# A language-model block on one core: the head reordered with all weights early, and the low part of the relu outputs read from PSUM after TensorE has subtracted the high part

## The reference

```
h = tok_W[x] * (x != 0) + pe[0 or 1, or zero for skipped pads]      # (2, 2048, 64)
a = layernorm(h) * g1 + b1;  q, k, v = split(a @ qkv_w + qkv_b)
p = softmax(q @ k.T + rel_bias) * scale                             # over 2048 positions
h = h + layernorm((p @ v) @ proj_w + proj_b) * g2 + b2
z = layernorm(h);  w = softmax over the top 2 of (z @ Wg + bg + bias)
y_e = relu(z @ W1[e] + b1[e]) @ W2[e] + b2[e]       for 8 experts, 64 -> 128 -> 64
out = h + sum_e w_e * y_e
```

## Time and profile before

| | |
|---|---|
| runs shown | 147.24, 149.72, 146.29 us; median 147.24 |
| profiled execution | 145.79 us, span of the trace 144.0 us |
| TensorE matmuls, busy in the span | 106.3 us (74%), 952 instructions |
| VectorE | 110.5 us (77%), 323 |
| ScalarE | 61.0 us (42%), 117 |
| GpSimd | 72.7 us (50%), 90 |

### The profile page before, as it was taken

The page is one execution under the profiler, slowest core; times in us unless marked ns, Lnnn a source line. Parts: engine busy times, 40 slices in busy tenths (PEclk is TensorE's granted clock), DMA queues, the critical chain, the costliest instruction groups (busy, mean ns, idle before and its releaser), DMA issues.

```text
span 144.0 us, 2642 instructions
## 1 busy us (share of the span) xinstructions
PE 106.3 (74%) x952; PEld 59.9 (42%) x952; DVE 110.5 (77%) x323; ACT 61.0 (42%) x117; POOL 72.7 (50%) x90
## 2 busy tenths in 40 slices
PE   0369982698987499699859679299839939829980
PEld 0133731552763276326524346145421624517650
DVE  7799699979407703279999999997999998799623
ACT  2372403103015021897959946276838605640020
POOL 2247928948000530759929995377597630360000
PEclk9999999555555555558999999956985775796555
DMA  3586000000000000000000000010000020003231
GB/s 61 178 282 230 0 2 5 0 1 0 0 0 0 0 7 0 0 2 0 7 0 0 0 5 0 0 36 0 5 0 0 2 41 0 0 0 65 49 73 36
DMA packets 5940, 3.91 MB, mean 27 GB/s; under 512 B 4675, under 2 KB 5031, under 8 KB 5928
## 3 DMA queue, kind: packets, MB, share of 16 engines
q1 hardware_dynamic: 5418, 3.45, 8.5%
q10 hardware_dynamic: 510, 0.31, 1.0%
HBM read 2.70 MB, written 1.06 MB: 26 GB/s over the span
## 4 chain that ended last, share of the span: by engine, by line
DVE 48%; PE 37%; issue 7%; ACT 2%; DMA 2%; POOL 1%; ACTq 0%; DVEq 0%
DVE acc L839 7%; DVE prod L832 5%; PE bank L1114 4%; PE bank L1094 4%; PE bank L1022 3%; PE bank L1019 3%; PE bank L941 2%; DMA w_tok<-in_token_w_dram 2%; DVE xs L798 2%; PE bank L1109 2%; PE bank L1119 2%; PE bank L901 2%; DVE xn L643 2%; DVE xs L797 2%; DVE og L782 2%
## 5 line engine op out<-in xcount | busy, mean ns | idle before, releaser
L324 POOL TENSOR_TENSOR hid_lo<-hid,hid_hi 128x512 f16<-128x512 f32 (+1 forms) x38 | 40.9, 1090 | 22.1 <-ACT hid_hi L570 21.8
L570 ACT ACTIVATE hid<-bank,b_col 128x512 f32<-128x512 f32 (+1 forms) x40 | 25.7, 646 | 26.7 <-PE bank L1094 26.5
L570 ACT ACTIVATE hid_hi<-bank,b_col 128x512 f16<-128x512 f32 (+1 forms) x38 | 24.4, 643 | 0.0
L1094 PE MATMUL bank<-xT,w_hi 128*128 128x512 f16 (+1 forms) x40 | 18.4, 461 | 0.9 <-ACT hid_hi L570 0.8
L839 DVE TENSOR_REDUCE acc<-prod 128x64 f32<-128x512 f32 x18 | 18.5, 1030 | 0.4
L1094 PE MATMUL bank<-xT,w_lo 128*128 128x512 f16 (+1 forms) x40 | 18.6, 465 | 0.0
L832 DVE TENSOR_TENSOR prod<-bank,comb 128x512 f32<-128x512 f32 x18 | 12.4, 688 | 6.3 <-PE bank L1119 5.9
L1114 PE MATMUL bank<-w_hi,hid_hi 128*128 128x64 f16 x144 | 13.6, 212 | 1.7 <-DVE hid_lo L324 1.7
L1114 PEld LDWEIGHTS bank<-w_hi,hid_hi 128*128 128x128 f16 x144 | 11.2, 109 | 7.5 <-issue 5.5
L1114 PE MATMUL bank<-w_lo,hid_hi 128*128 128x64 f16 x144 | 13.6, 212 | 0.0
L1109 PE MATMUL bank<-b_k,ones_b 3*128 3x512 bf16 x18 | 8.6, 476 | 6.6 <-DVE prod L832 5.1
(11 more groups left out here) (217 smaller groups left out, 223.5 us busy)
## 6 DMA issues: line engine op xcount, KB each, us to landing
ids_all<-ids_scratch SPq DMA_DIRECT2D x2, 512.0 KB, 4.6
w_sb<-in_w1g_dram SPq DMA_DIRECT2D x1, 516.0 KB, 6.3
hankel<-in_bias_table_dram SPq DMA_DIRECT2D x1, 512.0 KB, 4.3
out_dram<-looked SPq DMA_DIRECT2D x2, 256.0 KB
out_dram<-fin_all SPq DMA_DIRECT2D x3, 128.0 KB
w_sb<-in_w2b_dram SPq DMA_DIRECT2D x1, 260.0 KB, 6.1
...
```

Source lines behind the costliest of these rows:

```text
L324: return eng.tensor_tensor(hid_lo[:, k % 2, e, 0:m], hid[:, n % HSLOTS, 0:m], hid_hi[:, k % 2, e, 0:m], ALU.subtract)
L570: ins = act.activation(dst, bank[n % 2][:, 0:m], ACT.Relu, bias=b1_col[:, e:e + 1], scale=HSCALE / (XSCALE * XSCALE))
L1094: ins = mm(bank[n % 2][:, 0:m], w[:, HID * e:HID * (e + 1)], xT[:, k % 2, 0:m], start=part == 0, stop=part == 1)
```

## The change

Five things, cut to their core below.

1. The low part of the experts' relu. ScalarE writes the high part first, from the sum in PSUM scaled down by KEEP = 1 - 2^-11 so that it never lies above the full value (`high`). TensorE subtracts it from the same bank by a matmul with a negative scaled identity (`take_high`), and ScalarE applies the relu to what is left in PSUM, in 16 bits (`low`). `hid` and all subtractions of `low` on GpSimd and VectorE go. Each `first_layer(n)` ends with `take_high(n - 1)`, each `hidden(n)` with `low(n - 1)`; three banks are in turn where there were two.
2. The order of the head on TensorE: `project_values` first, `weights` in pieces between the steps of the pair table and unit 0, all four tiles' weights and scores ahead of unit 1's attended values. M_BANK changes so that tiles 2 and 3 have banks 7 and 6.
3. The suffix sums of the skip counts come from 16 matmuls on shifted columns in place of one matmul and a scan.
4. The split of w1: ScalarE scales and rounds it (`w1_high`), GpSimd only subtracts, in four pieces. `bias_parts` works on 8 partitions x 64 in place of 1 x 512, is first on GpSimd, and its result is loaded by three DMAs in place of one.
5. The loads of w1, w2 and b2 go ahead of that of the early ids; `early_one_hots` on VectorE goes from before `split_exps` to after `key_part(1)`.

```diff
-HSLOTS = 6
+KEEP = 1.0 - 2.0 ** -11
+LBANKS = 3
...
-        M_BANK = [7, 2, 2, 2]
+        M_BANK = [7, 2, 7, 6]
...
+            sp.dma_start(w1_sb[:], w1g).then_inc(loads["w1"], 16)
+            sp.dma_start(w2_sb[:], w2b1).then_inc(loads["w2"], 16)
+            sp.dma_start(b2_row[:], b2).then_inc(loads["b2"], 16)
             sp.dma_start(ids_by_seq[:, :, 0:FIRST], ids_dram[:, 0:FIRST].partition_broadcast(P)).then_inc(loads["ids_early"], 16)
-            sp.dma_start(w1_sb[:], w1g).then_inc(loads["w1"], 16)
-            sp.dma_start(b2_row[:], b2).then_inc(loads["b2"], 16)
-            sp.dma_start(w2_sb[:], w2b1).then_inc(loads["w2"], 16)
             sp.wait_ge(s_b2p, 1)
-            sp.dma_start(b2_k[:], b2_part[:]).then_inc(loads["b2_k"], 16)
+            for part in range(3):
+                sp.dma_start(b2_k[part:part + 1, :], b2_part[:, part, :]).then_inc(loads["b2_k"], 16)
...
+            bias_parts(); table_values(); w1_parts(); rsqrt1(0); rsqrt2(0); w2_parts(); rsqrt1(1); rsqrt2(1)
+            rsqrt1(2); rsqrt2(2); rsqrt1(3); rsqrt2(3); fin_parts(0); fin_parts(1); fin_parts(2)
+            fin_parts(3); fin_parts(4); rsqrt1(4); rsqrt2(4)
...
+            def w1_high():
+                act.wait_ge(loads["w2"], 16)
+                act.mul(b1_col[:], w2_sb[:, EXPERTS * D:], HSCALE)
+                act.mul(b1_down[:], w2_sb[:, EXPERTS * D:], HSCALE * KEEP)
+                act.wait_ge(loads["w1"], 16)
+                act.mul(w1_sb[:], w1_sb[:], XSCALE).then_inc(s_w1h, 1)
+                act.wait_ge(s_w1h, 1)
+                act.copy(w1_hi[:], w1_sb[:]).then_inc(s_w1h, 1)
...
+            def high(k, e):
...
                 act.wait_ge(s_z, n + 1)
-                if n >= HSLOTS:
-                    wait_lo(act, n - HSLOTS)
...
+                act.activation(hid_hi[:, k % 2, e, 0:m], bank[n % LBANKS][:, 0:m], ACT.Relu, bias=b1_down[:, e:e + 1],
+                               scale=KEEP * HSCALE / (XSCALE * XSCALE)).then_inc(s_high, 1)
+
+            def low(k, e):
+                n = EXPERTS * k + e
+                act.wait_ge(s_rest, n + 1)
+                m = P * SIZE[k]
+                act.activation(hid_lo[:, k % 2, e, 0:m], bank[n % LBANKS][:, 0:m], ACT.Relu, bias=b1_col[:, e:e + 1],
+                               scale=HSCALE / (XSCALE * XSCALE)).then_inc(s_hid, 1)
+
+            def hidden(k, e):
+                high(k, e)
+                if k or e:
+                    n = EXPERTS * k + e - 1
+                    low(n // EXPERTS, n % EXPERTS)
...
+            read_v(); count_late(0); count_late(1); w1_high(); pair_exps(); read_turned_exps(); squares(0)
+            score_tile(0); score_tile(1); read_turned(0); hidden(0, 0); choice_exp(0); hidden(0, 1); squares(1)
+            hidden(0, 2); score_tile(2); hidden(0, 3); score_tile(3); hidden(0, 4); hidden(0, 5); squares(2)
...
             def read_k():
+                dve.tensor_scalar(minus_h[:], ident[:], -XSCALE * XSCALE / HSCALE, None, ALU.mult)
...
-                link(dve.tensor_tensor_scan(sk_suf[:, ::-1], skc[:, ::-1], skc[:, ::-1], 0.0, ALU.add, ALU.bypass))
-                dve.tensor_scalar(sk_flat[:], sk_suf[:, 1:1 + JBLK], flat, None, ALU.mult)
...
             def flat_weights():
                 dve.wait_ge(s_toe, 1)
                 dve.tensor_scalar(flat_w[:], cnt_half[:, :, 0:2], flat, None, ALU.mult)
+                dve.tensor_scalar(sk_flat[:], sk_suf[:, 1:1 + JBLK], flat, None, ALU.mult)
...
-                link(dve.tensor_copy(hid_hi[:, k % 2, e, 0:P * SIZE[k]], hid[:, n % HSLOTS, 0:P * SIZE[k]]))
-                low_part(dve, k, e).then_inc(s_lo_d, 1)
...
+            one_hot_rows(0, JBLK); skip_blocks(); late_one_hots(); read_k(); toeplitz_low(1); values()
+            read_counts(); skip_columns(); penalties(); flat_weights(); row_maxima()
+            split_exps(); rows_a(0); rows_b(0); rows_b2(0); skip_key(); key_part(0); rows_c(0)
+            skip_key_rows(); key_part(1); early_one_hots(); choose_a(0); choose_b(0); rows_a(1); rows_b(1)
+            rows_b2(1); key_part(2); rows_c(1); key_part(3); rows_a(2); choose_a(1); rows_b(2); rows_b2(2); weigh(0)
...
+                for d in range(ROWS):
+                    ins = mm(bank[1][:, 8:8 + ROWS - d], ones_b[:], skip_j[:, d:], start=d == 0, stop=d == ROWS - 1,
+                             skip_group_check=True)
...
-                if n < 2:
-                    pe_.wait_ge(*((s_idcol, 1), (s_skTsb, 1))[n])
+                if n < LBANKS:
+                    pe_.wait_ge(*((s_idcol, 1), (s_skTsb, 1), (s_p, 2))[n])
                 else:
-                    pe_.wait_ge(s_hid, n - 1)
+                    pe_.wait_ge(s_hid, n + 1 - LBANKS)
...
                 ins.then_inc(s_z, 1)
+                if n:
+                    take_high(n - 1)
+
+            def take_high(n):
+                k, e = n // EXPERTS, n % EXPERTS
+                m = P * SIZE[k]
+                pe_.wait_ge(s_high, n + 1)
+                mm(bank[n % LBANKS][:, 0:m], minus_h[:], hid_hi[:, k % 2, e, 0:m], start=False, stop=True,
+                   skip_group_check=True).then_inc(s_rest, 1)
...
-                if i == 0 and LO_DVE[k]:
-                    wait_lo(pe_, EXPERTS * k + LO_DVE[k][-1])
...
-                if i == 0:
-                    wait_lo(pe_, EXPERTS * k + LO_POOL[k][-1])
...
+            project_values(); counts(); pair_scores(); weights(0, 0, 2); pair_penalties(); weights(0, 2, 4)
+            embed(0); weights(1, 0, 2); turn_exps(); weights(1, 2, 4); attend(0, 2); skip_weights()
+            skip_scores(); scores(0); weights(1, 4, 8); scores(1); weights(3, 0, 4); embed(1); skip_turn()
+            weights(3, 4, 8); turn(0); gate(0); first_layer(0, 0); first_layer(0, 1); attend(2, 4)
+            first_layer(0, 2); weights(2, 0, 2); scores(2); first_layer(0, 3); weights(2, 2, 4); scores(3)
+            first_layer(0, 4); embed(2); first_layer(0, 5); attend(6, 4); first_layer(0, 6); turn(1); gate(1)
+            first_layer(0, 7); first_layer(1, 0); first_layer(1, 1); second_layer(0); first_layer(1, 2)
...
-            first_layer(4, 7); second_layer(14); second_layer(15); second_layer(16); look_up(1)
+            first_layer(4, 7); take_high(EXPERTS * UNITS - 1); second_layer(14); second_layer(15); second_layer(16); look_up(1)
```

117 lines of the change are left out of this document (35 added, 82 removed).

## The result

| | before | after |
|---|---|---|
| median of the runs | 147.09 us (4 runs, 146.29 to 149.72) | 128.36 us (4 runs, 127.58 to 132.16) |
| after to before | | 0.8725, 95% interval 0.8633 to 0.8816 |
| span of the profiled execution | 144.0 us | 125.6 us |
| mean granted clock over the span | 0.740 | 0.919 |

The kernel is faster by 12.8%. The forecast was 124.0 in a range of 114 to 136; the time lies in it, 4.4 us above the forecast. The four executions of the kernel after run from 127.58 us at a mean clock of 0.919 to 132.16 at 0.875; where the clock touches a comparison, the text gives it.

The account below looks back on a forecast made before the run. The prediction took TensorE at half clock to bound B and VectorE, stretched by GpSimd's subtractions, to bound C. Gains of 3.3 + 9.0 + 9.7 + 1.0 = 23.0 us gave a span of 121.0, forecast as 124 us, range 114 to 136.

Parts of the forecast that it names:

- Stage A: From the start until VectorE starts the variance of unit 0, 28.2 us; 3.3 us gained, bounds 0 and 5.
- L710's stall: Before the penalties, a multiply took 2.17 us behind GpSimd's split of w1; some 2.0 of it would go.
- The cover for `w1_high`: ScalarE's 7.15 us of idle before the exponentials would hide its 3 us of new work, under 1 us to spare.
- Stage B: From unit 0's variance until TensorE turns unit 1: TensorE work at half rate, 32.0 us to 23.0, 9.0 gained.
- The clock check: A sign for stage B: granted clock above 0.8 between the scores and turn(1), with turn(1) near 48.
- rival 1: The head stays at the lower clock level: stage B gives 0 instead of 9.0, about 133 us; chance 15%.
- Stage C: From TensorE turning unit 1 until VectorE weighs block 14, bound by VectorE: 70.2 us to 60.5, 9.7 gained.
- the coupling: In stage C, two nearly full engines, VectorE and TensorE, coupled by 18 handovers lose some: 4 us added.
- rival 4: TensorE keeps at the upper clock level in stages C (54 us) and D (10 us): about 115 us; chance 13%.
- Rival 2, the ring,: An expert's high, take_high and low run one after another, 2.6 us an expert: 145, or 150 to 170; chance 6%.
- Rival 3: VectorE does not get faster without GpSimd, the long rows having another cause: about 132 us; chance 6%.
- Stage D: From VectorE weighing block 14 to the end, 13.6 us; 1.0 us gained, bounds 0 and 4.7.

Follow-up runs that it names:

- run 1: The changed kernel with 38 subtractions of the old shapes put back on GpSimd, on tiles nothing else uses: 142.13 us, ratio to before 0.9814.
- Run 6: The changed kernel with GpSimd's four w1 subtractions waiting until VectorE has split the exponentials: 126.9 us, ratio to before 0.8654.
- run 8: The changed kernel with TensorE's subtraction of the high part done in two matmuls of half the weight each: 130.54 us, ratio to before 0.8894.
- run 10: The changed kernel with run 6's wait and weights(3, 4, 8) moved into the two gaps behind turn(0): 124.98 us, ratio to before 0.8615.
- run 11: The kernel of run 10 with weights(1, 4, 6) moved ahead of skip_scores, four wide matmuls among the one-column ones: 126.18 us.
- Run 9: The changed kernel with the weighing and summing over experts 4 to 7 left out on VectorE: 123.68 us, ratio to before 0.8456.
- run 4: The changed kernel with two banks for the experts' first layer in place of three: 153.62 us, ratio to before 1.0521.
- run 5: The two-bank kernel of run 4 with each low pass directly behind its high pass, and three last-expert subtractions taken earlier: 143.79 us, ratio to before 0.9833.
- run 3: The kernel before with only the new low part (high, take_high, low) added, on two banks, with the old head and orders: 155.95 us.

## Why the prediction came out as it did

**What bounds the kernel before: right.** B as TensorE work at the lower clock and C as a stretched VectorE both held as readings of the kernel before; run 1 shows the second by itself.

**Stage A: the step that failed is where L710's stall went.** "That split is partly moved to ScalarE and starts later, so some 2.0 of it goes" took the stall off one operation and did not ask which one would stand beside the subtractions next. It was the negation of the row maxima, on the path, at the same price: 2.00 us. The check set for it, exponentials near 20, failed at 23.36. Run 6 gives the stall back, to 21.50, and of it 0.8 us at the end of A. The other 1.3 of the 2.1 missed are the forecast's own worry about pieces of `weights` at the slower pace, named there at up to 1.7. It came true: the penalties, written at 19.18, were multiplied at 20.04 behind one piece, and in run 6 the exponentials, done at 22.4, were turned at 23.59 behind another. The cover for `w1_high` held: ScalarE did it from 15.57 on, in two passes of 1.05 each, and then waited 5.66 us.

**Stage B: the step that failed is its size, 9.0 for 2.7.** The clock check passed (0.83, above 0.8) and turn(1) stood at 56.3 all the same, not near 48. Two terms were mis-sized.
First, "TensorE's 26.9 busy us would be 13.5 at the upper level" halved everything. TensorE's groups by form in B of after, with the mean duration of one (before had 426 and 238 ns for the first two, all at the lower level, and 161 to 186 for the one-column ones):

```profile
L1012 PE MATMUL bank<-vp,pT 128*128 128x65 f32 x16 | 3.5, 303 | 0.0
...
L994 PE MATMUL bank<-h_part,oneh_t 128*128 128x64 bf16 x24 | 2.1, 196 | 0.0
...
L974 PE MATMUL bank<-eg_hi,oneh_t 128*128 128x1 f16 x8 | 1.4, 175 | 0.0
```

These durations overlap, so what a queue pays is the distance from one start to the next. From the starts in the traces of before and after, at the lower and the upper level: 0.43 and 0.22 us for 512 columns, 0.30 and 0.18 for the 65-column ones in 32 bits, 0.090 and 0.064 for 64 columns, 0.072 and 0.066 for one. With these, B's 26.9 us of before would be 16.6 at the upper level (my estimate), 3.1 more than the 13.5. The 65-column ones make the largest part of it, 9.6 of the 26.9.
Second, the clock: 10.2 of 29.3 us at the lower level, where I had none. At half a us for each (run 8) that is 5.0. The two make 8.1; the 2.1 us by which I had rounded up, 23.0 for a sum of 20.9, took a part of them back, which leaves 6.0 of the 6.3 missed. My choice between "upper level for certain" and rival 1's "half of B slow" had put 85% on the first, and the trace lies between the two.
The rule weighed in the prediction, the Trainium skill's "TensorE: Matmul & The Clock Gate", section "Why this matters for your kernels", sustained work for the full rate and gaps that lose it, is again not what the trace shows in its first half: between 41.5 and 50.7 TensorE had no gap, and the clock fell in the middle. Two gaps of 0.46 and 0.41 us stand shortly before, but run 10 has none from 26.0 to 45.9 us and two falls. What made it fall stays open: run 11's change didn't stop the first fall, run 8 was without it for no reason in the program, and the spells in B lasted 3.4 to 10.2 us in kernels whose work there is the same.

**Stage C: the gain is right, the sum behind it only in part.** That GpSimd's subtractions would stop stretching VectorE was right, row by row: 49.8 us forecast, 48.81 measured. But the sum took C as the fuller of VectorE and TensorE, plus 4 us of coupling, and two errors in it cancel. "56.4 us at the same mean clock" took 0.81 over from before, where the clock was 0.97 and TensorE busy 48.84 us; and the coupling, the time beyond the fuller engine, was 8.8 us, not 4. Run 9 shows that neither engine's sum sets this stage: 10.1 us less of VectorE shortened it by 1.0. Of the 2.9 us by which C beat the forecast, some 2 are this execution's clock; at 0.91 C is 59.5 (run 6). That is luck, and it is the C of rival 4 in part (54), which I had at 13%. VectorE was 85% busy and the short `xn`, `xs`, `sel` rows came as listed. The high passes are under 1.2 us apart in 15 of 31 cases, mostly 1.14 to 1.16, and 1.65 on average. ScalarE's low passes do not appear among those that waited for a subtraction; the waits of second_layer for low parts are 1.3 us in all. GpSimd at 27.1 us was a little above the 25 set.

**Rival 2, the ring,** was put at 6% with "three banks and the one-expert lag in both queues" against it. The lag was no argument: in run 4 it is what makes two banks so dear, 1.96 us an expert, and without it (run 5) they cost 1.75. The number of banks carried it: with three, the densest stretches went at ScalarE's own pace of 1.14, above the 0.87 of the ring as I had it. (Its 145 us is mis-added: 83 us for C in place of 60.5 makes 147, still outside the range.) I had not seen in the prediction that this makes the low path worthless without the new head (run 3).

**Rival 3** is out: VectorE did get faster, and run 1 slows it again. **Stage D** gained 1.9 for 1.0, its clock being 0.72 instead of 0.51; the last block still ends it, at the lower level.

**In all:** 23.0 forecast, 18.4 measured; the misses, 2.1 + 6.3 - 2.9 - 0.9 = 4.6, are the distance. The time fell into the range because its ends had been made for such a case, not because B was understood, and it came as near as 4.4 us because C erred the other way.
